# First attention stage of a six-layer chain: score products four at a time, the mask added on VectorE, and a new order of work around one shared PSUM bank

## The reference, cut to what matters

```python
q, k, v = LN(x) @ Wq.T + bq, ctx @ Wk.T + bk, ctx @ Wv.T + bv      # split into 16 heads of 8
scores = einsum('bhqd,bhkd->bhqk', q, k) / sqrt(8)
scores = where(mask == 0, -inf, scores)                            # mask: 32 x 257, the same for all batches
out = einsum('bhqk,bhkd->bhqd', softmax(scores), v)                # heads joined again
x = x + out @ Wo.T + bo
```

## Time and profile before

| | us |
|---|---|
| median of 3 runs | 2129.08 |
| profiled execution, its own time | 2125.4 |
| span of its trace | 2123.6 |
| first add_out of the stage to its last, 32 tiles | 68.9 to 705.0 |
| busy PE / DVE / ACT / POOL over the whole span | 1705.6 / 1418.0 / 968.1 / 477.9 |

### The profile page before, as it was taken

The page is one execution under the profiler, slowest core; times in us unless marked ns, Lnnn a source line. Parts: engine busy times, 40 slices in busy tenths (PEclk is TensorE's granted clock), DMA queues, the critical chain, the costliest instruction groups (busy, mean ns, idle before and its releaser), DMA issues. The chain is left out here.

```text
span 2123.6 us, 37416 instructions
## 1 busy us (share of the span) xinstructions
PE 1705.6 (80%) x11541; PEld 1100.6 (52%) x11568; DVE 1418.0 (67%) x3093; ACT 968.1 (46%) x2622; POOL 477.9 (23%) x497
## 2 busy tenths in 40 slices
PE   5999999999999399878889585577777734499998
PEld 3666666666666155445555474465565624244443
DVE  3666666666666366657677444799999975577776
ACT  2555555555555133323233235899999901011110
POOL 0111111111111010000000011688888843000000
PEclk9999999999999699989989798798989966699999
DMA  3101010010100550000056100000000000100000
GB/s 80 31 20 30 20 30 27 23 30 20 30 20 11 169 165 0 16 6 0 0 167 197 61 0 0 1 1 0 1 1 0 0 10 0 46 6 6 10 6 15
DMA packets 69410, 66.57 MB, mean 31 GB/s; under 512 B 5753, under 2 KB 66896, under 8 KB 69328
## 3 DMA queue, kind: packets, MB, share of 16 engines
q1 hardware_dynamic: 66516, 64.00, 9.9%
q10 hardware_dynamic: 2812, 1.66, 0.3%
HBM read 61.45 MB, written 4.19 MB: 31 GB/s over the span
## 5 line engine op out<-in xcount | busy, mean ns | idle before, releaser
L1836 PE MATMUL ss_y_ps<-ss_h,ss_diag 128*128 128x256 f32 x1024 | 265.2, 423 | 133.0 <-ACT sc_dt L1754 93.5
L418 ACT ACTIVATE x_probs<-x_s_ps,x_neg_max 128x257 f32<-128x257 f32 x512 | 238.4, 471 | 251.3 <-DVE x_neg_max L489 251.3
L1836 PEld LDWEIGHTS ss_y_ps<-ss_h,ss_diag 128*128 128x128 f32 x1024 | 216.4, 214 | 181.5 <-issue 90.7
L489 DVE TENSOR_REDUCE x_neg_max<-x_s_ps 128x2 f32<-128x514 f32 x256 | 174.3, 681 | 179.2 <-PE x_s_ps L288 179.2
L1738 ACT ACTIVATE ss_decay<-sc_dt,sc_a 128x256 f32 (+1 forms) x496 | 206.2, 466 | 1.8 <-DVE ss_h L1801 1.8
L496 DVE COPY x_pT<-x_pT_ps 128x512 f32<-128x512 f32 x256 | 175.5, 686 | 42.6 <-PE x_pT_ps L298 38.4
L285 PE MATMUL x_s_ps<-x_kT,x_qblk 32*128 32x257 f32 x1024 | 182.6, 433 | 0.0
L1792 DVE SCALAR_TENSOR_TENSOR ss_decay<-ss_decay,ss_h 128x1024 f32<-128x1024 f32 x124 | 152.4, 1229 | 29.3 <-ACT ss_decay L1738 29.1
L298 PE MATMUL x_pT_ps<-all_ident,x_probs 128*128 128x128 f32 x1024 | 169.9, 289 | 0.6 <-ACT x_probs L418 0.5
L1748 ACT ACTIVATE ss_come<-ss_dtu,sc_xd 128x256 f32<-128x256 f32 x384 | 162.7, 502 | 6.6 <-POOL ss_dtu L1694 6.6
L1708 POOL TENSOR_TENSOR ss_diag<-all_ident,sc_xd 128x512 f32<-128x512 f32 x128 | 160.7, 1256 | 11.4 <-PE ss_y_ps L1836 1.4
(11 more groups left out here) (357 smaller groups left out, 3223.3 us busy)
## 6 DMA issues: line engine op xcount, KB each, us to landing
x_ctx_t<-ctxT SPq DMA_DIRECT2D x48, 514.0 KB, 3.8
kept_ctx_t<-ctxT SPq DMA_DIRECT2D x16, 514.0 KB, 8.3
kept_ctx_n<-ctx SPq DMA_DIRECT2D x16, 512.0 KB, 8.7
x_ctx_n<-ctx SPq DMA_DIRECT2D x16, 512.0 KB, 3.9
all_x<-x SPq DMA_DIRECT2D x4, 512.0 KB, 7.1
x_mid<-all_x SPq DMA_DIRECT2D x32, 64.0 KB, 3.6
all_x<-x_mid SPq DMA_DIRECT2D x4, 512.0 KB, 7.5
out<-all_x SPq DMA_DIRECT2D x8, 256.0 KB, 2.1
```

Source lines behind the costliest of these rows:

```text
L418: ins = nc.scalar.activation(probs[p][:, n, :], s_ps[u % 2][:, j, 0:S2], ACT.Exp, bias=neg_max[p][:, n:n + 1], accum_out=sums[p][:, n:n + 1])
L489: vec.tensor_reduce(neg_max[p][:, 2 * u:2 * u + 2], s_ps[u % 2][:, :, 0:S2], AX.X, ALU.max, negate=True).then_inc(max_sb, 1)
L1836: ins = nc.tensor.matmul(y_ps[p][:, 0:DI], diag[q][:, m, :], h[q][:, m, :], start=(q == 0 and m == 0), stop=(q == NQ - 1 and m == NH - 1))
```

## The change

Four things, all in `stage_cross0`:

1. `scores` runs in even slots only and makes all four groups of a batch at once, on the four bands of 32 rows, into one PSUM tensor of four banks (`s_ps`), which isn't double-buffered: it waits until the maximum pass over the batch before has ended (`max_sb`). The mask products and `onehot`, with its load, are gone.
2. The maximum pass is four `tensor_tensor_reduce` per batch: each reads a product from PSUM and the float32 mask from SBUF, writes -(score + mask) to `probs` and the minimum to `neg_max`. In the built program each of them is two instructions (below). `exps` reads `probs` instead of PSUM, with scale -1, in place.
3. `turn(u - 2)` runs in slot u instead of `turn(u - 1)`, and `attend` stands behind it in odd slots.
4. The fills of the shared bank stand in a new order, one or two to a slot, and the copies of `xnT` and `qT` move from DVE to ACT, in front of the exponentials. The last row's values get a fill of their own (`fill_vtail`, `copy_vtail`).

```diff
+        mask_b = sb("mask_b", [P, S2])
+        s_ps = ps("s_ps", [P, CH, BANK])
...
-            def scores(t, p, u):
...
-                for j in range(2):
-                    ins = mm(s_ps[u % 2][:, j, 0:S2], onehot[rows[j], :], mask_b[rows[j], :], start=False, stop=True)
+            def scores(t, p, b):
...
+                if not (isinstance(t, int) and t == 0 and b == 0):
+                    pe.wait_ge(max_sb, (t * BT + b) * CH)
+                for c in range(CH):
+                    q = slice(S * c, S * c + S)
+                    ins = mm(s_ps[:, c, 0:S2], qblk[p][q, b * P:(b + 1) * P], kT[p][q, b * S2:(b + 1) * S2], start=True, stop=True)
...
+            def fill_even(t, p, u, prev, nxt):
+                if u == 0 and (prev or nxt):
+                    pe.wait_ge(v_sb, t * 2 + 1)
+                    if nxt:
+                        fill_xnT(t + 1)
+                    if prev:
+                        fill_ptail(t - 1, 1 - p)
+                if u == 2 and nxt:
+                    pe.wait_ge(v_sb, t * 2 + 2)
+                    fill_qT(t + 1)
+                    fill_tails(t + 1, 1 - p)
+                if u == 4 and prev:
+                    if nxt:
+                        pe.wait_ge(k_sb, t * 2 + 3)
+                    fill_r(t - 1)
+                if u == 6 and prev:
+                    if nxt:
+                        pe.wait_ge(k_sb, t * 2 + 4)
+                        fill_vtail(t + 1)
+                    fill_out(t - 1)
...
+            def fill_odd(t, p, u, prev, nxt):
+                if u == 1:
...
+                    if prev:
+                        pe.wait_ge(ptail_sb, t)
+                    fill_v(t, p, 1)
+                if u == 3:
+                    if prev:
+                        attend_tail(t - 1, 1 - p)
+                    if nxt:
+                        pe.wait_ge(q_sb, t + 2)
+                        fill_k(t + 1, 1 - p, 0)
+                if u == 5 and nxt:
+                    if prev:
+                        pe.wait_ge(on_sb, t)
+                    fill_k(t + 1, 1 - p, 1)
+                if u == 7 and nxt:
+                    if prev:
+                        pe.wait_ge(x_sb, t)
+                    pe.wait_ge(vtail_sb, t + 2)
+                    fill_v(t + 1, 1 - p, 0)
...
-            fill_v(0, 0, 1)
...
             def exps(t, p, u):
-                act.wait_ge(max_sb, t * UN + u + 1)
+                act.wait_ge(max_sb, (t * UN + u) * 2 + 2)
...
-                    ins = nc.scalar.activation(probs[p][:, n, :], s_ps[u % 2][:, j, 0:S2], ACT.Exp,
+                    ins = nc.scalar.activation(probs[p][:, n, :], probs[p][:, n, :], ACT.Exp, scale=-1.0,
...
-            def maxes(t, p, u):
-                dve.wait_ge(scores_psum, t * UN + u + 1)
-                vec.tensor_reduce(neg_max[p][:, 2 * u:2 * u + 2], s_ps[u % 2][:, :, 0:S2], AX.X, ALU.max,
-                                  negate=True).then_inc(max_sb, 1)
+            def maxes(t, p, b):
+
+                dve.wait_ge(scores_psum, t * BT + b + 1)
+                dve.sem_inc(waited_dve, 1)
+                for c in range(CH):
+                    n = b * CH + c
+                    vec.tensor_tensor_reduce(probs[p][:, n, :], s_ps[:, c, 0:S2], mask_b[:, :], -1.0, -MASKED,
+                                             ALU.add, ALU.min, neg_max[p][:, n:n + 1]).then_inc(max_sb, 1)
...
             def tile(t, p, prev, nxt):
-                if nxt:
-                    norm(t + 1)
                 for u in range(UN):
-                    maxes(t, p, u)
...
+                    if u == 0 and nxt:
+                        norm(t + 1)
+                    if u % 2 == 0:
+                        maxes(t, p, u // 2)
                     if u == 0 and prev:
...
                         if nxt:
-                            copy_xnT(t + 1)
-                        if prev:
-                            copy_ptail(t - 1)
-                            recip(t - 1, 1 - p)
...
+                            dve.wait_ge(xnT_sb, t + 2)
+                        copy_ptail(t - 1)
+                        recip(t - 1, 1 - p)
...
+                    if u == 4 and prev:
                         normalise(t - 1)
...
+                    if u == 6 and prev:
+                        add_out(t - 1)
+                    if u == 6 and nxt:
+                        copy_vtail(t + 1, 1 - p)
+                    if u >= 2:
+                        copy_pT(t, u - 2)
```

More of the change, by code:

```diff
@@ L147, in stage_cross0 @@
         lnw = sb("lnw", [P, 4, T])
-        s_ps = [ps(f"s_ps{p}", [P, 2, BANK]) for p in range(2)]
+        s_ps = ps("s_ps", [P, CH, BANK])
         pT_ps = [ps(f"pT_ps{p}", [P, BANK]) for p in range(2)]
@@ L335, in fill_out @@
                 ins.then_inc(out_psum, 1)
+            def fill_even(t, p, u, prev, nxt):
[18 more added lines that the diff above has]
+                    fill_out(t - 1)
+                if u == 6 and nxt and not prev:
+                    pe.wait_ge(k_sb, t * 2 + 4)
+                    fill_vtail(t + 1)
@@ L366, in tile @@
-                    if u == 4 and nxt:
-                        if prev:
-                            pe.wait_ge(x_sb, t)
-                        pe.wait_ge(q_sb, t + 2)
-                        fill_k(t + 1, 1 - p, 0)
-                    if u == 5 and nxt:
-                        fill_k(t + 1, 1 - p, 1)
-                    if u == 6 and nxt:
-                        fill_v(t + 1, 1 - p, 0)
-                    if u == 7 and nxt:
-                        fill_v(t + 1, 1 - p, 1)
+                    if u % 2 == 0:
+                        scores(t, p, u // 2)
@@ new lines, in tile @@
+                    if u >= 2:
+                        turn(t, p, u - 2)
+                    elif prev:
+                        turn(t - 1, 1 - p, UN - 2 + u)
+                    if u % 2 == 0:
+                        fill_even(t, p, u, prev, nxt)
+                        continue
+                    if u >= 5:
+                        attend(t, p, (u - 5) // 2)
+                    elif prev:
+                        attend(t - 1, 1 - p, (u + 3) // 2)
+                    fill_odd(t, p, u, prev, nxt)
@@ L393, in _ @@
             tile(T - 1, 1, True, False)
+            pe.wait_ge(x_sb, T - 1)
+            turn(T - 1, 1, UN - 2)
+            fill_ptail(T - 1, 1)
             turn(T - 1, 1, UN - 1)
+            attend(T - 1, 1, BT - 2)
             attend(T - 1, 1, BT - 1)
-            pe.wait_ge(x_sb, T - 1)
-            fill_ptail(1)
-            pe.wait_ge(ptail_sb, T)
+            attend_tail(T - 1, 1)
             fill_r(T - 1)
-            attend_tail(T - 1, 1)
             fill_out(T - 1)
@@ L414, in exps, with copy_xnT, copy_q @@
             def exps(t, p, u):
-                act.wait_ge(max_sb, t * UN + u + 1)
+                act.wait_ge(max_sb, (t * UN + u) * 2 + 2)
                 for j in range(2):
                     n = 2 * u + j
-                    ins = nc.scalar.activation(probs[p][:, n, :], s_ps[u % 2][:, j, 0:S2], ACT.Exp,
+                    ins = nc.scalar.activation(probs[p][:, n, :], probs[p][:, n, :], ACT.Exp, scale=-1.0,
                                                bias=neg_max[p][:, n:n + 1], accum_out=sums[p][:, n:n + 1])
                 ins.then_inc(exp_sb, 1)
+            def copy_xnT(t):
+                act.wait_ge(xnT_psum, t + 1)
+                nc.scalar.activation(xnT[:, :], m_ps[:, 0:P], ACT.Copy).then_inc(xnT_sb, 1)
+            def copy_q(t):
+                if not (isinstance(t, int) and t == 0):
+                    act.wait_ge(qblk_sb, t)
+                act.wait_ge(qT_psum, t + 1)
+                nc.scalar.activation(qT[:, :], m_ps[:, P:2 * P], ACT.Identity, bias=cols[:, 0:1]).then_inc(q_sb, 1)
             def copy_o(t):
@@ L568, in _ @@
             vec.tensor_tensor(out_bias[:, :], m_ps[:, 0:D], bo_b[:, :], ALU.add).then_inc(prep_dve, 1)
-            copy_xnT(0)
-            dve.wait_ge(tails_psum, 1)
-            copy_q(0)
+            dve.wait_ge(q_sb, 1)
             copy_tails(0, 0)
+            copy_vtail(0, 0)
             tile(0, 0, False, True)
@@ L577, in _ @@
             tile(T - 1, 1, True, False)
+            copy_ptail(T - 1)
+            copy_pT(T - 1, UN - 2)
             copy_pT(T - 1, UN - 1)
-            copy_ptail(T - 1)
             recip(T - 1, 1)
```

125 lines of the change are left out of this document (49 added, 76 removed).

## The result

| | before | after |
|---|---|---|
| median, us | 2129.06 (4 runs, 2127.22 to 2129.67) | **2021.38** (4 runs, 2020.38 to 2024.68) |
| profiled execution, us | 2125.4 | 2024.68 |
| start of the stage's last add_out, us from the span's start | 705.0 | 599.0 |
| from there to the end of the span, us | 1418.6 | 1423.9 |

The ratio is 0.9501, with an interval from 0.949 to 0.9513: 5% less time. All of it lies in the first stage, which ends 106.0 us earlier. The other five stages took 5.3 us more in this one execution.

What follows compares the result with a forecast made beforehand. PE's own queue bounds the first stage at 20.71 us a tile; 16.5 of work plus waits of 0.69 and 0.48 gives 17.7. 32 x (20.71 - 17.7) = 96, plus 5 at the ends, gives 2027 us, range 2004 to 2064.

Steps and rivals of the forecast that it cites:

- The score block, -3.3 us a tile: On PE: four four-band blocks of 0.65 us replace eight of 0.74, saving 3.3 us a tile.
- PE without waits: PE's own work per tile after the change: 20.71 - 3.3 - 0.87 = 16.5 us.
- The wait before `fill_r`: PE's 0.87 us wait a tile for GpSimd's sums goes, as this fill moves two slots behind them.
- The pair, e = 0.42: On DVE: one maximum pass plus reading out its minimum occupies the queue for 0.42 us, bounds 0.34 and 0.61.
- the rival of the free read-out: On DVE: reading out the minimum hides in the overlap, e below 0.36; at 0.34, T = 17.1, 2008 us; chance 0.06.
- VectorE's start: VectorE's first maximum pass starts 0.81 us behind the start of PE's score block.
- The two waits, 0.69 and 0.48: PE waits 0.69 us at slot 1's `fill_v` for `copy_ptail` and 0.48 at slot 5's `fill_k` for `normalise`.
- the point from which the change would be slower: On DVE: at e = 0.69 a tile takes 20.7 us, so the change would stop gaining.
- The ends, 5 us with bounds 0 to 8: Outside the steady tiles: about 2 from one `fill_v`, about 2 from low-clock score blocks, about 1 from the closing chain.
- Half rate: On DVE: two float32 sources make a pass 0.68 us; e = 0.79 gives T = 22.4, 2179 us; chance 0.05.
- Two by two: On PE: four bands run in twos, score block grows by 0.43; T = 19.4, 2082 us; chance 0.02.
- The clock: PE falls to 1.2 GHz at the new waits; over 30 us a tile, 300 us slower or more; chance 0.02.

Runs made afterwards that it cites:

- widened kernel: Changed kernel with the last value row's stationary tensor padded with zeros from 16 to 128 columns; 2012.91 us, ratio 0.9461.
- doubled kernel: Changed kernel with every maximum pass made twice, first into spare tensors, so VectorE's queue grows by four pairs a batch; 2194.4 us, ratio 1.0318.
- kernel with blocks of two: Changed kernel's order kept, but each batch's four score products made in two blocks of two bands; 2098.01 us, ratio 0.9855.
- earlier copies: Changed kernel with `copy_ptail` and `normalise` in slots 0 and 4 behind three of the four maximum pairs; alone 2001.04 us, ratio 0.9404.

## Why the prediction was right, and where its terms were off

2027 was forecast, 2021.4 came, and a tile takes 17.66 us where I had 17.7. The steps:

- **The score block, -3.3 us a tile, was right.** The block is 0.65 us to the hundredth. PE without waits is 17.66 - 0.62 - 0.46 = 16.58, forecast 16.5.
- **The wait before `fill_r` went**, as said.
- **The pair, e = 0.42, was too dear: it is 0.347,** just above the lower bound of 0.34. This is the term on which I had said the rest turns. I leaned on ACT, whose read-out of 0.19 fills the overlap between two passes. VectorE's takes 83 ns and lies inside that overlap whole. By my own sum this alone would have given 17.1, the rival of the free read-out, and its 2008 us. That rival held on its mechanism (I gave it 0.06), and the forecast held on the time, which is luck: errors of the other sign made up for this one.
- **What filled the gap in the waits.** The pair took 8 x 0.073 = 0.58 off them. VectorE's start, 0.94 behind the block and not 0.81, put 0.26 back. PE reaches each wait 0.06 sooner than I had it (2.46 and 2.68 us behind the score block): 0.12. And from the end of the copy to the start of the fill it is 0.08 and 0.13, not 0.05: 0.11. Together 1.17 - 0.58 + 0.49 = 1.08.
- **The gaps around the 16-column fill** cost 0.29 a tile by the widened kernel, and my sum had moved this fill at no cost. They are part of the 16.58, which came out within 0.1 of the forecast all the same, so about 0.25 elsewhere in PE's work went the other way. Less than 0.1 of that is the waiting of the kernel before, 0.93 to 0.96 a tile where I took off 0.87; the rest isn't traced.
- **The two waits, 0.69 and 0.48, are 0.62 and 0.46,** in their places and behind the two DVE instructions that I named. None at slots 3 and 7. The doubled kernel shows that each grows by four pairs. That kernel is also the test of the point from which the change would be slower: at e = 0.69 its tile takes 21.74 at full clock, where my sum gives 20.9 (I had written 20.7), so that point lies lower than 0.69.
- **The ends, 5 us with bounds 0 to 8, are 8.4,** just outside the bounds, and they lie elsewhere than I had them. The first tile ends 5.1 us sooner (68.9 to 63.8), of which 3.05 is one period: 2.0 where I expected 4. The last two tiles take 23.2 us (575.8 to 599.0) in place of 35.6 (669.4 to 705.0), of which 6.1 are two periods: 6.3 where I expected 1.
- **Half rate did not come.** The pass takes 423 ns for 257 columns with two float32 sources, one of them in PSUM, as long as the plain maximum. The Trainium skill's "Vector Engine (DVE) Microarchitecture Reference", section "Points that are easy to get wrong", halves the throughput of a two-tensor form whose two sources are both in SBUF and not bf16. This trace has a pass with such a read-out only with one source in PSUM, and shows no halving there.
- **Two by two did not come:** the block of four takes 0.65 and not the 1.08 of that rival. The clock stayed at 1.00 in the stage, and PE waited for no exponentials. The kernel with blocks of two is not quite this rival: it adds whole blocks at 0.83, with load and drains, where the rival added 0.43 of streaming.
- **PE remained the bound, and what was lost was lost to VectorE's emptying of PSUM.** The 0.96 us a tile of waiting stands before two such copies, and putting them one pass earlier took 0.68 of it. The Trainium skill's "TensorEngine Tiling (Array Packing)", section "Performance Considerations", warns that the emptying of PSUM may become the bottleneck once tiling has made TensorE faster. The trace agrees in part: the waits stand there, but PE is busy for 94.5% of the window and VectorE for 73.7%, so the emptying did not become the bottleneck.
- **Two side sums do not come out as written.** With e = 0.36 and ends of 8 the low end is 2009 and not 2004, and the half rate with a hidden read-out gives 2124 and not 2121. Neither touches the forecast.

I did not see that the mask pass, on which I spent most of the working, brings nothing here. My sum took the mask's share of the eight old blocks and the new waits together; it was never set up against a version with four bands and the mask on PE, where that share is 4 x 0.11 and the waits are 0.24. Only with the earlier copies does it pay: 16.68 against 17.96 us a tile.

## What to carry to other kernels

Price a change part by part against the other combinations, not only against the kernel before: of the three parts here the bands of one block are worth 2.42 us a tile, the order 0.55, and the mask pass 0.08 in the old order, -0.29 in the new one, and 1.28 in the new one with the earlier copies and the wide fill. Where engines walk a fixed order, the wait of one is set by all that stands ahead of the copy it needs; a copy that another engine waits for goes as early as the buffers behind it allow, and a pass that frees the buffers is what allows it. And count the changes of tile shape along PE's queue, and not the columns alone: a fill of 16 columns between fills of 128 cost 0.29 us more than the same fill padded with zeros to 128.
